# Disentangled attention with a routed feed-forward part on one core: value products placed ahead of scores, row maxima turned by VectorE, three units' loads issued in the projection stage, and the third norm applied to the logits

## The reference, cut to what matters

```python
# disentangled attention: q, k, v of (4 batches, 16 heads, 1024 rows, 16 numbers)
pos_k  = rel_embeddings @ Wk + bk                        # 128 relative positions, per head
scores = q @ k.T / scale                                 # scale = sqrt(16 * 3)
c2p    = take_along_axis(q @ pos_k.T, clip(rel + 64))    # rel: log buckets of i - j
p2c    = take_along_axis(k @ pos_k.T, clip(-rel + 64)).swapaxes(-1, -2)
probs  = softmax(scores + (c2p + p2c) / scale)
ctx    = probs @ v
att    = layernorm(ctx @ Wo + bo + h, 1e-7) * ln_scale + ln_bias
# around it: h = layernorm(x); x2 = x + layernorm(att)
# feed-forward part: 8 experts of 256 -> 1024 -> 256, one chosen for each token
r   = layernorm(x2)
e   = argmax(softmax(r @ Wr + br))
y   = sum over i of relu((r if e == i else 0) @ W1[i] + b1[i]) @ W2[i] + b2[i]
out = x2 + layernorm(y)
```

## Time and profile before

| | before |
|---|---|
| time of three runs | 1784.40, 1785.49 (median), 1792.77 us |
| profiled execution | 1794.4 us, its span 1792.3 us |
| busy over the span: PE, DVE, ACT, POOL | 90%, 76%, 64%, 58% |
| mean granted TensorE clock | 0.946 of full speed |
| DMA | 421.65 MB, mean 235 GB/s |
| PE, DVE busy in 200 to 1260 us | 1020 and 953 of 1060 us |

### The profile page before, as it was taken

How to read it: one execution, slowest core, us unless ns; L and a number is a source line. 1 busy time by engine, 2 the same in 40 slices (tenths; PEclk the granted TensorE clock), 3 DMA queues, 4 the chain that set the end, 5 groups by cost and what they waited for, 6 DMA issues and landing times. The chain is left out here.

```text
span 1792.3 us, 41887 instructions
## 1 busy us (share of the span) xinstructions
PE 1615.2 (90%) x13688; PEld 1147.8 (64%) x13688; DVE 1364.4 (76%) x3868; ACT 1145.8 (64%) x2764; POOL 1030.9 (58%) x1264
## 2 busy tenths in 40 slices
PE   7963799999999999999999999999977866999997
PEld 4531566666666666666666666666634646999996
DVE  4753798999998999898899998999956754555553
ACT  6852587877877888878777878787754631222221
POOL 0003776777776777777777777777814622333332
PEclk9985899999999999999999999999997857999998
DMA  4986788878888788788888887888608616666762
GB/s 136 332 284 221 246 278 275 273 264 267 269 280 275 261 275 279 256 272 286 269 265 267 268 274 260 273 264 281 211 25 220 190 65 197 194 193 198 206 202 57
DMA packets 292450, 421.65 MB, mean 235 GB/s; under 512 B 35382, under 2 KB 233804, under 8 KB 292139
## 3 DMA queue, kind: packets, MB, share of 16 engines
q1 hardware_dynamic: 271640, 378.99, 65.2%
q10 hardware_dynamic: 16851, 30.67, 5.6%
q0 software_dynamic: 3744, 9.31, 1.4%
HBM read 241.39 MB, written 177.79 MB: 234 GB/s over the span
## 5 line engine op out<-in xcount | busy, mean ns | idle before, releaser
L934 ACT ACTIVATE t_probsT<-t_flip 128x512 f32<-128x512 f32 x1024 | 603.2, 615 | 192.3 <-PE t_flip L791 103.3
L851 DVE TENSOR_REDUCE t_most<-t_scores 128x1 f32<-128x640 f32 (+1 forms) x512 | 435.7, 851 | 120.1 <-PE t_scores L775 119.4
L997 POOL TENSOR_TENSOR t_near<-t_near,masks 128x384 f32<-128x384 f32 (+1 forms) x128 | 146.5, 1144 | 275.5 <-DMA t_near<-skew_d 274.8
L861 DVE CUSTOM_DVE_ANT_0 t_band<-t_scores,t_near,t_most 128x384 f32<-128x384 f32 (+1 forms) x512 | 297.0, 580 | 0.5 <-DVE t_most L851 0.2
L872 DVE TENSOR_SCALAR_CACHE_REDUCE t_band<-t_band,t_top 128x384 f32<-128x384 f32 (+1 forms) x512 | 291.2, 569 | 0.0
L926 ACT COPY t_table<-t_table_ps 128x388 f32<-128x388 f32 x502 | 251.2, 500 | 54.1 <-PE t_table_ps L747 50.9
L812 PE MATMUL t_sum_ps<-t_probsT,vals 128*32 128x256 f32 x4096 | 274.3, 385 | 0.3 <-ACT t_probsT L934 0.3
L1013 POOL TENSOR_TENSOR t_near<-t_near,masks 128x768 f32<-128x768 f32 (+1 forms) x128 | 268.6, 2098 | 0.0
L775 PE MATMUL t_scores<-masks,t_near 128*128 128x128 f32 x1408 | 244.8, 278 | 19.6 <-POOLq L1016 18.8
L798 PE MATMUL t_flip<-masks,t_band 128*128 128x128 f32 x1408 | 258.1, 274 | 0.0
L768 PE MATMUL t_scores<-afters,quests 105*128 105x256 bf16 (+3 forms) x1024 | 244.3, 288 | 3.8 <-DVE t_top L861 3.6
(11 more groups left out here) (212 smaller groups left out, 2572.4 us busy)
## 6 DMA issues: line engine op xcount, KB each, us to landing
skew_d<-t_table SPq DMA_DIRECT2D x128, 1024.0 KB, 11.3
t_near<-skew_d SPq DMA_DIRECT2D x128, 640.0 KB, 8.0
t_near<-skew_d SPq DMA_DIRECT2D x128, 384.0 KB, 7.4
e_w<-in_L_ffn_W_dram ACTq DMA_DIRECT2D x39, 512.0 KB
e_w<-in_L_ffn_W_dram SPq DMA_DIRECT2D x39, 512.0 KB
split_d<-p_part SPq DMA_DIRECT2D x32, 384.0 KB, 3.3
afters<-split_d SPq DMA_DIRECT2D x128, 96.0 KB
quests<-split_d SPq DMA_DIRECT2D x128, 96.0 KB
```

The source lines that it names most:

```text
L851: nc.vector.tensor_reduce(most[:, c:c + 1], out[:, wide:S], AX.X, ALU.max).then_inc(far_seen, 1)
L861: nc.vector.tensor_tensor_reduce(band[n % 2][:, t, 0:wide], out[:, 0:wide], near[n % 2][:, 0, t, at:at + wide], 1.0, most[:, c:c + 1], ALU ...
L934: nc.scalar.activation(probsT[s % 4][:, half * 512:(half + 1) * 512], flip_ps[half][:, :], ACT.Exp, scale=SCALE).then_inc(expd, 1)
```

## The change

Four edits.

1. In attention PE's step issues `weigh` between `make_table` and `score`, not after the second flip.
2. The maxima are turned by DVE: four 32x32 transposes after `look(s)` at s % 8 == 1, from a part tile padded to 32 columns, straight into t_topT. PE's L820 and ACT's L946 are gone, with `ident16`, and ACT issues the DMA at the end of its step s % 8 == 2 instead of 1.
3. The third unit's loads are issued by SP in the projection stage (EARLY = 3), and Wo is loaded in attention (u == 12) with a semaphore of its own.
4. In mix PE's first projection waits for Wo and the bias alone. The third norm is not applied: x2 itself is turned and multiplied with Wr, and the logits are scaled by each row's inverse and shifted by the row's shift times the column sums of Wr (PE with ones, into m_aside_ps). b1 is loaded in rows and turned by PE. The statistics of norms 0 and 1 stand in PSUM (m_mv). The turning comes six steps after its group's first step instead of nine.

```diff
-EARLY = 2
+EARLY = 3
...
                 if s == 5:
                     hats.load_unit(sp, split_d, 1)
                 if s == 6:
+                    hats.load_unit(sp, split_d, 2)
+                if s == 7:
                     hats.load_far(sp, far_d, 0)
...
-            def turn_top(n):
-                pe.wait_ge(split_made, 5 * (n + 1))
-                pe.wait_ge(table_kept, by_act(min(n * QT + QT + AHEAD + 2, TS) - 1))
-                nc.tensor.matmul(table_ps[0:PARTS * QT, 0, 0:P],
-                                 top_part[n % 2][:, :, :].rearrange("p a t -> p (a t)"), ident16[:, :],
-                                 start=True, stop=True).then_inc(top_turned, 1)
-
             for s in range(-AHEAD, TS + LAG + 1):
                 back = s - LAG
                 if live(back):
                     flip(back, 0)
                 if live(s + AHEAD):
                     make_table(s + AHEAD)
+                if live(back - 1) and back % 2 == 0:
+                    weigh(back - 2)
+                    weigh(back - 1)
                 if live(s):
                     score(s)
                 if live(back):
                     flip(back, 1)
-                if live(back - 1) and back % 2 == 0:
-                    weigh(back - 2)
-                    weigh(back - 1)
-                if s > QT and s % QT == 1 and s // QT <= N:
...
-            nc.vector.tensor_copy(ident16[:, :], masks[:, 4, :]).then_inc(ident_made, 1)
+            def turn_top(n):
+                dve.wait_ge(split_made, 5 * (n + 1))
+                if n < 2:
+                    dve.wait_ge(parts_set, 2)
+                if n >= 2:
+                    dve.wait_ge(top_in[(n - 2) % BUFS], 16 * ((n - 2) // BUFS + 1))
+                for a in range(4):
+                    last = nc.vector.transpose(topT[n % 2][:, 32 * a:32 * a + 32],
+                                               top_part[n % 2][32 * a:32 * a + 32, :, :].rearrange("p a t -> p (a t)"))
+                last.then_inc(top_turned, 1)
...
             for s in range(TS):
                 look(s)
+                if s > QT and s % QT == 1:
+                    turn_top(s // QT - 1)
                 if s >= BEHIND and (s - BEHIND) % QT == 0:
                     normalise((s - BEHIND) // QT)
             level(TS - 1)
+            turn_top(N - 1)
...
-            def keep_top(n):
+            def send_top(n):
                 act.wait_ge(top_turned, n + 1)
-                if n >= 2:
-                    act.wait_ge(top_in[(n - 2) % BUFS], 16 * ((n - 2) // BUFS + 1))
-                nc.scalar.copy(topT[n % 2][:, :], table_ps[0:PARTS * QT, 0, 0:P]).then_inc(top_kept, 1)
-                act.wait_ge(top_kept, n + 1)
-                nc.scalar.dma_start(quest[n % BUFS][MROW:ROWS, :], topT[n % 2][:, :]).then_inc(top_in[n % BUFS], 16)
+                nc.scalar.dma_start(quest[n % BUFS][MROW:ROWS, :], topT[n % 2][0:PARTS * QT, :]).then_inc(top_in[n % BUFS], 16)
...
-                if s > QT and s % QT == 1 and s // QT <= N:
-                    keep_top(s // QT - 1)
+                if s > QT and s % QT == 2 and s // QT <= N:
+                    send_top(s // QT - 1)
...
-        stats, mv = sb("stats", [P, 2, 3, G, 6]), sb("mv", [P, 2, 3, G, 2])
-        root, inv, shift = (sb(w, [P, 2, 3, G]) for w in ("root", "inv", "shift"))
+        stats, mv = sb("stats", [P, 2, 3, G, 6]), ps("mv", [P, 2, 2, G, 2])
+        root, inv, shift = (sb(w, [P, 2, 2, G]) for w in ("root", "inv", "shift"))
+        row_mv = sb("row_mv", [P, NT, 2])
+        row_root, row_inv, row_shift = (sb(w, [P, NT]) for w in ("row_root", "row_inv", "row_shift"))
+        wr_sum, offset = sb("wr_sum", [P, E]), sb("offset", [P, NT, E])
+        b1_rows, aside_ps = sb("b1_rows", [E * KC, P]), ps("aside_ps", [P, E * KC + E])
         out_ps = [ps(f"out_ps{i}", [P, G, D]) for i in range(2)]
...
-            loads = [(wo[:, :, :], Wo.rearrange("(k p) n -> p k n", p=P)),
-                     (ls_b[:, :], row(ln_s, D)), (lb_b[:, :], row(ln_b, D)),
+            loads = [(ls_b[:, :], row(ln_s, D)), (lb_b[:, :], row(ln_b, D)),
                      (wr[:, :, :], Wr.rearrange("(k p) n -> p k n", p=P)),
                      (br_b[:, :], row(br, E)), (steps[:, :], c_steps)]
...
-                for i in range(lo, hi):
+                if hi > 2:
+                    g = s - 2 * LAG
+                    for t in range(G):
+                        last = nc.vector.bn_aggr(row_mv[:, g * G + t, :], stats[:, c, 2, t, :])
+                    last.then_inc(row_mv_made, 1)
+                if s >= NORMED:
+                    continue
+                for i in range(lo, min(hi, 2)):
                     for t in range(G):
                         last = nc.vector.bn_aggr(mv[:, c, i, t, :], stats[:, c, i, t, :])
                 last.then_inc(mv_made, 1)
                 if s + 1 < NG:
                     residual(s + 1)
                 dve.wait_ge(root_made, s + 1)
...
+            dve.wait_ge(row_root_made, 1)
+            nc.vector.reciprocal(row_inv[:, :], row_root[:, :]).then_inc(row_norm, 1)
+            dve.wait_ge(row_norm, 1)
+            nc.vector.scalar_tensor_tensor(row_shift[:, :], row_mv[:, :, 0], -1.0, row_inv[:, :], ALU.mult, ALU.mult
+                                           ).then_inc(row_norm, 1)
+            dve.wait_ge(row_norm, 2)
+            nc.vector.tensor_tensor(offset[:, :, :], wr_sum[:, :].unsqueeze(1).to_broadcast([P, NT, E]),
+                                    row_shift[:, :].unsqueeze(2).to_broadcast([P, NT, E]), ALU.mult).then_inc(row_norm, 1)
+            dve.wait_ge(row_norm, 3)
+            nc.vector.tensor_tensor(offset[:, :, :], offset[:, :, :], br_b[:, :].unsqueeze(1).to_broadcast([P, NT, E]), ALU.add
+                                    ).then_inc(row_norm, 1)
+            dve.wait_ge(row_norm, 4)
             dve.wait_ge(logit_made, NG)
             link(nc.vector.tensor_tensor(logits[:, :, :], logit_ps[:, 0:NT * E].rearrange("p (t e) -> p t e", e=E),
-                                         br_b[:, :].unsqueeze(1).to_broadcast([P, NT, E]), ALU.add))
+                                         row_inv[:, :].unsqueeze(2).to_broadcast([P, NT, E]), ALU.mult))
+            link(nc.vector.tensor_tensor(logits[:, :, :], logits[:, :, :], offset[:, :, :], ALU.add))
...
-            for s in range(STEPS):
+            for s in range(NORMED):
...
+                if s >= TURN:
+                    keep_xf(s - TURN)
                 act.wait_ge(shift_made, s + 1)
-                for i in range(lo, hi):
+                for i in range(lo, min(hi, 2)):
                     g = s - LAG * i
-                    src, dst = ((y1, y4), (y4, y5), (x2, xf))[i]
+                    src, dst = ((y1, y4), (y4, y5))[i]
                     if i == 1 and g >= BUFS:
                         act.wait_ge(x2_made, g - BUFS + 1)
-                    if i == 2 and g >= BUFS:
-                        act.wait_ge(xf_turned, g - BUFS + 1)
                     for t in range(G):
                         last = nc.scalar.activation(dst[g % BUFS][:, t, :], src[g % BUFS][:, t, :], ACT.Identity,
                                                     bias=shift[:, c, i, t:t + 1], scale=inv[:, c, i, t:t + 1])
                     last.then_inc(norm_made[i], 1)
-            keep_xf(NG - 1)
+            for g in range(NORMED - TURN, NG):
+                keep_xf(g)
+            act.wait_ge(row_mv_made, NG)
+            nc.scalar.activation(row_root[:, :], row_mv[:, :, 1], ACT.Sqrt, bias=eps[:, 1:2]).then_inc(row_root_made, 1)
...
-            pe.wait_ge(loaded, 16 * 6)
+            pe.wait_ge(wo_in, 16)
             pe.wait_ge(bo_made, 7)
             project_out(0)
-            for s in range(STEPS + 2):
+            for s in range(NG + TURN + 1):
                 if s + 1 < NG:
                     project_out(s + 1)
-                g = s - 2 * LAG - 1
+                if s == 2:
+                    pe.wait_ge(loaded, 16 * 5)
+                    pe.wait_ge(const_in, 48)
+                    nc.tensor.transpose(aside_ps[:, 0:E * KC], b1_rows[:, :], ident[0:E * KC, 0:E * KC])
+                    for k in range(2):
+                        last = nc.tensor.matmul(aside_ps[:, E * KC:E * KC + E], masks[:, 3, :], wr[:, k, :],
+                                                start=(k == 0), stop=(k == 1))
+                    last.then_inc(aside_made, 1)
+                g = s - TURN
```

76 lines of the change are left out of this document (42 added, 34 removed).

## The result

| | before | after |
|---|---|---|
| time, median | 1787.93 us (4 runs, 1784.4 to 1792.77) | 1861.61 us (4 runs, 1854.79 to 1870.99) |
| ratio to before | | 1.0414, 95% interval 1.0356 to 1.0472 |
| profiled span | 1792.3 us | 1863.7 us |
| unit of attention | 17.81 us | 19.26 us |
| SyncE's first issue of mix (bias rows) to the logits | 1339.78 to 1456.94, 117.2 us | 1424.05 to 1528.43, 104.4 us |

The prediction was 1767 us, between 1745 and 1815. The time lies where rival C had put it, 1862, at a chance of 0.09. The attention's loss of some 84 us hides a gain of 13 us in mix.

The account below looks back on a forecast made before the run. A few DMA engines, as much as TensorE, were taken to hold attention. Profiled 1794.4 - 17.5 (mix) - 4.5 (loads) + 3 (attention) + 1 (its end) = 1776.4, less 8.9 for the median: 1767 us, range 1745 to 1815.

Parts of the forecast that it names:

- rival C: Attention: the delay of the maxima's DMA stays at 5.1 us or over, units 19.4 and more, 1862 us; chance 0.09.
- What bounds attention: Attention: a few DMA engines, never idle and carrying more than the others, hold it as much as TensorE; units 17.81 us.
- Edit 1: Attention, value products ahead of scores: taken as 0, with -0.5 to +0.5 us a unit as bounds.
- Edit 2, the transposes: Attention, VectorE: four transposes of the maxima cost between 0.1 and 1.8 us a unit, taken as 0.4.
- The ring: Attention: flip, value products, score, VectorE, transposes and next DMA issue wait on each other; 14.3 us plus the DMA's delay.
- L: Attention: delay of the maxima's DMA from its issue on, up to 5.1 us, taken as 3.5.
- Edit 3: Loads moved into projection: 4.5 us saved at attention's start, bounds 3 and 9; 0 cost in projection, +3 if not hidden.
- Edit 4: Mix: earlier start, shorter steps and shorter tail save 17.5 us together, between 10 and 24.
- start: Mix: the first projection starts once the bias is ready, not after the last small load; 4.0 us saved.
- tail: Mix, GpSimd's last addition to the logits: 9.6 us halves, one more link costs 0.45; 4.4 us saved, bounds 2 and 6.
- full-clock steps: Mix: a step of 4.90 us loses two activations from its ring, 1.17 us at most, taken as 0.75.
- the 12 steps: Mix: the steps where three norms run, over which 0.75 us a step gives 9 us, bounds 4 and 14.

Follow-up runs that it names:

- x13: Edits 3 and 4 alone, with value products over half of their columns from the third unit on (output not the reference's): 1764.6 us, 0.9860 of before.
- x14: Edits 3 and 4 alone, with q and k loads cut to 16 of 48 rows from the seventh unit on (output not the reference's): 1744.0 us.
- x17: Edits 3 and 4 alone, with q and k parts stored row by row in DRAM, same bytes and issues: 1752.5 us, 0.9794 of before.
- x5: The changed kernel with edits 1 and 2 undone, so edits 3 and 4 alone: 1765.5 us, 0.9866 of before.
- x1: The kernel before with edit 1 alone: 1815.9 us, 1.0151 of before.
- x4: The changed kernel with edit 2 undone, so edits 1, 3 and 4: 1796.4 us, 1.0032 of before.
- x9: The changed kernel, with the maxima's DMA going to a spare tile and no flip waiting for it (output not the reference's): 1778.3 us, 0.9934 of before.
- x10: The changed kernel with edit 1 undone, maxima's DMA to a spare tile and no flip waiting for it (output not the reference's): 1771.8 us, 0.9900 of before.
- x2: The kernel before with edit 2 alone: 1847.1 us, 1.0330 of before.
- x3: The changed kernel with edit 1 undone, so edits 2, 3 and 4: 1819.9 us, 1.0162 of before.
- x15: Edits 2, 3 and 4, with skewed table reads cut to some half of their tiles from the third unit on (output not the reference's): 1778.5 us.
- x16: Edits 2, 3 and 4, with q and k loads cut to 16 of 48 rows from the seventh unit on (output not the reference's): 1788.1 us.
- x18: Edits 2, 3 and 4, with q and k parts stored row by row in DRAM: 1810.4 us, 1.0135 of before.

## Why the prediction was wrong, step by step

- **What bounds attention** (a few DMA engines, not TensorE): right in part. x13 excludes TensorE at 17.77, and x14 and x17 shorten the unit by relieving few engines, but only by 0.33 and 0.21 us. What holds it at 17.4 to 17.6 then is open: no run took work off VectorE, which is busy 16.0 us of a unit, and in x17 the flips wait again for the maxima's DMA (17.2 us in 34 units, against 1.3 in x5). One reading was wrong besides: not some 8 us of a unit have all 16 DMA engines busy. The mean share of 0.82 in the earlier trace rows already says more, and by the packet records it is over 0.9 in 66% of the half microseconds from 300 to 1200 us, 11.8 us a unit. By the rule of the Trainium skill (DMA: Bandwidth & Descriptors, section Why a DMA increments its semaphore by 16 and not by 1), the number of engines is the largest up to 16 that divides both slowest dimensions, so these loads use three with 3 and 48 and sixteen with 16 and 48. The trace agrees, with at most three of their packets at once but for 3% of the time in x5 and up to sixteen in x17, and the writes beside them land in 7.8 us instead of 11.2.
- **Edit 1** (0, with -0.5 to +0.5 a unit): inside its bounds and outside the value taken. It cost 0.38 alone (x1), 0.43 with edits 3 and 4 (x4 to x5), 0.24 without wait and cast (x9 to x10). Shown in the trace are 0.10 us more from table products to value products, four times a unit, and in x1 a wait for the cast, 20.5 us in 47 of about 49 units. The two come to about 0.8 a unit, more than the 0.38, so something else got shorter; what did is open. The prediction forgot what follows a moved piece: the value products had covered the cast.
- **Edit 2, the transposes** (0.4 us): 0.83.
- **The ring** (14.3 us without the delay): right. From the late flip to the next send 14.29 us go by in the unit shown and in the median of the 46 units from 300 to 1200 us, and 14.6 in their mean, since some units take up to 16.2. It also exists in the order of before: in x2 the same way takes 13.3 us in the median and 13.7 in the mean, about one pair of value products (1.0) less. The prediction said nothing of x2; the expectation's 12.6 to 13.3 holds the median at its upper end.
- **The step that failed: the delay.** "Longer units give the few engines time to drain, which shortens L, so the ring should settle near 17.8 to 18.3", and the 3.5 taken from a queue "at its shortest" because the reads start behind it. From the send to the last packet 4.18 us go by in the mean, and from there to the flip 0.6 more (in the unit shown 0.4: 736.72 + 4.81 = 741.53, flip at 741.96), which the 3.5 lacked. So L measured 4.8 and not 3.5, and with the ring's 14.6 that makes the 19.4 of these 46 units.
  The feedback that the prediction counted on does exist, but it doesn't settle. After a unit longer than the median the next delay is 3.6 us in the mean, after a shorter one 4.7. A short delay makes a short unit, and after a short unit the reads stand close ahead of the send again. In a row the delays are 5.0, 3.4, 4.8, 4.1, 4.9, 3.2 us.
  What the delay goes with is how long before the send the last pair of table reads was issued, counted from the first of the two (mean delay of such units in us, and how many they are):

  | reads ahead of the send by | changed kernel | x3 | x15, half of the reads | x16, a third of the loads | x18, parts by row |
  |---|---|---|---|---|---|
  | 3 to 4 us | 4.7 (15) | 4.6 (23) | 2.6 (11) | 4.9 (6) | 4.9 (17) |
  | 5 to 6 us | 2.5 (6) | 2.8 (4) | 1.6 (4) | 2.4 (26) | 2.3 (25) |

  The prediction had the reads behind the send; the ring carries them round with it, and now they stand 2 to 5.5 us ahead. At 3 to 4 us leaving out some half of the reads takes 2 us off the delay, while relieving the few engines takes nothing off (4.9 against 4.6 in x3; at 5 to 6 us 2.3 and 2.4 against 2.8). So here the reads ahead make most of the delay, and the loads on few engines little of it; x16 and x18 have lower means because more of their units have the reads 5 us or more ahead. This holds for units in which the flip waits. In the order of before the delay is 5.2 us with the reads 3.1 us behind the send, and what makes it there is open. x15 is the only run that took from the reads, and none changed when they are issued.
- **The time of rival C** (1862) was met to the microsecond by luck. C had a ring of 14.3 and an L of 5.1 with 21 us won outside the units; measured were 14.6, 4.8 and some 13 us.
- **Edit 3** (4.5 us): first maxima 5.3 us sooner in x5, though the loads held up projection by 1.4 us, where the prediction took 0 (first table write after it at 142.91 against 141.48).
- **Edit 4** (17.5 us): 12.8 us in the changed kernel's profile, 20.3 in x5's (1332.16 to 1429.02). Over all profiles the same stretch is 113.8 to 117.2 us without edit 4 (4 profiles) and 91.7 to 107.1 with it (16). The parts were sized well: start 4.1 (4.0 forecast), tail 9.6 to 4.6 (5.0 saved, 4.4 forecast), full-clock steps 4.90 to 3.97 (0.93 saved, 0.75 forecast). In this stage LAG is 2, so that the turning moved from five steps behind its group to four, and not from nine to six as the text on the change has it; the 12 steps of the prediction are counted rightly. The shift had taken 0.17 us at 1407.31, where GpSimd stood still, and 1.22 us at 1418.20 beside it. With m_mv in PSUM it takes 161 ns at 1510.38 with GpSimd busy. The rule of the Trainium skill (SBUF — State Buffer, section Who interferes with whom), that a VectorE operation with two inputs in SBUF contends with a GpSimd operation that reads SBUF, agrees with that. What differs between the two profiles is how long TensorE runs at 1.2 GHz: from 1470 to 1490 us the changed kernel has a granted clock of 0.50, and steps of 7.1 us.
- **Sum.** Edits 3 and 4: -22 forecast, x5 against before -24. Attention: +3 forecast; +84 measured up to SyncE's first issue of mix (1424.05 - 1339.78), +91 by its 63 units.

## What to carry to other kernels

Before moving a send later, add up the ring that it closes, from the waiting instruction round to the send, and add the delay that the trace shows now up to the waiting instruction, not the delay hoped for once things are slower. Then look at the delay unit by unit: a mean can stand between two values that take turns. A transfer's queue neighbours are part of the ring: if they are issued by the same steps, a longer period shifts them with it and may put them ahead. Where a short burst of loads stands on few engines, change the layout in DRAM before cutting the transfer into pieces, since pieces cost issues.

## What the runs showed that was not expected

A 6 KB transfer takes 4 us to its first packet while others are busy (median first packet 4.05 us before, 3.93 after), and 1.4 us at attention's end with idle queues. Cutting four loads into twelve cost 53 us though the writes beside them landed 4 us sooner (x11 against x5, on two chips). One step more of lag between scores and flips cost 176 us (x7 against the changed kernel); the step of the value products moved with it, and the cause is open.
